# Two transformer layers on one core: order of the q/k remainders, score products and end-of-batch work in the first layer's attention

## The reference

```python
xn = layernorm(x)
# layer 0 attention: 16 heads of width 64
q, k, v = einsum('qdh,bcd->bhcq', Q, xn)*sq, einsum(..., K, xn)*sq, einsum(..., V, xn)*sv
p = softmax(causal(q @ k.T / 64))
z = einsum('dvh,bhcv->bcd', W, p @ v) * (sqrt(2) / 16)
# layer 0 ffn: a shared expert and 32 routed ones, the best 6 of a token weighted
f = sum_e comb[t, e] * (silu(xn @ gate_e.T) * (xn @ up_e.T)) @ down_e.T + shared(xn)
x = x + z + f
# layer 1: attention with 4 heads of width 32, and three 128-wide quantized
# linear blocks with layernorm and gelu
x = x + attn1(layernorm(x)) + ffn1(layernorm(x))
```

## Time and profile before

| what | value |
|---|---|
| median of 3 runs | 1194.93 us (1194.64 to 1196.25) |
| the profiled execution's own time | 1196.25 us |
| its span, first to last instruction | 1194.4 us |
| TensorE busy | 1173.1 us, 98% |
| VectorE busy | 981.5 us, 82% |
| ScalarE busy | 810.0 us, 68% |
| GpSimd busy | 405.4 us, 34% |
| mean granted TensorE clock | 0.997 of full speed |

### The profile page before, as it was taken

One profiled execution on the slowest core, in us unless ns is written; L12 is line 12 of the kernel. 1 busy time (PEld: TensorE's weight loads), 2 busy tenths in 40 slices (PEclk: granted clock), 3 DMA queues, 4 the chain that ended last, 5 costly groups with the idle time before them and its releaser, 6 DMA issues.

```text
span 1194.4 us, 23821 instructions
## 1 busy us (share of the span) xinstructions
PE 1173.1 (98%) x8908; PEld 898.2 (75%) x8908; DVE 981.5 (82%) x1918; ACT 810.0 (68%) x2182; POOL 405.4 (34%) x364
## 2 busy tenths in 40 slices
PE   8999999999999999999999999999999999999998
PEld 6777687767776777677767777777777777767866
DVE  5988588869886989698969886988797878988886
ACT  6885577557755775677567755775577668767775
POOL 1326420640064007300630064006400768526820
PEclk9999999999999999999999999999999999999999
DMA  7004200320031004100410041004100410000000
GB/s 261 2 30 144 90 1 30 125 62 2 30 125 63 1 30 128 60 1 30 131 56 2 30 134 54 2 30 134 53 2 30 144 43 2 10 10 19 1 11 28
DMA packets 44292, 63.93 MB, mean 54 GB/s; under 512 B 8144, under 2 KB 18384, under 8 KB 43920
## 3 DMA queue, kind: packets, MB, share of 16 engines
q1 hardware_dynamic: 44176, 62.39, 16.3%
HBM read 59.48 MB, written 2.88 MB: 52 GB/s over the span
## 4 chain that ended last, share of the span: by engine, by line
PE 81%; DVE 9%; ACT 4%; issue 2%; DMA 1%; POOL 1%; SPq 1%; DVEq 0%; POOLq 0%; ACTq 0%
PE psum L1507 14%; PE psum L1529 12%; PE psum L1454 12%; PE psum L65 10%; PE psum L67 9%; PE psum L66 9%; PE psum L1564 4%; DVE mneg L1146 3%; ACT probs L766 3%; PE psum L1464 2%; PE psum L1753 2%; PE psum L1533 1%; PE psum L1816 1%; DVE qk_lo L1126 1%; PE psum L1406 1%
## 5 line engine op out<-in xcount | busy, mean ns | idle before, releaser
L766 ACT ACTIVATE probs<-psum,mneg 128x256 f32<-128x256 f32 (+3 forms) x528 | 253.0, 495 | 166.3 <-DVE mneg L1146 165.4
L1146 DVE TENSOR_REDUCE mneg<-psum 128x2 f32<-128x1024 f32 (+2 forms) x320 | 245.2, 819 | 46.4 <-PE psum L1464 44.0
L1137 DVE COPY pt<-psum 128x512 f32<-128x512 f32 x320 | 204.8, 681 | 42.3 <-PE psum L1507 40.4
L1507 PE MATMUL psum<-ident,probs 128*128 128x128 f32 x1600 | 210.0, 277 | 3.9 <-DVE pt L1137 1.6
L1507 PEld LDWEIGHTS psum<-ident,probs 128*128 128x128 f32 x1600 | 177.1, 141 | 31.8 <-ACT probs L766 13.7
L573 POOL TENSOR_TENSOR qk_lo<-sg,qk_hi 128x512 fp32r<-128x512 f32 x64 | 91.8, 1441 | 163.0 <-ACT qk_hi L820 163.0
L1529 PE MATMUL psum<-pt,v_all 128*64 128x384 f32 (+5 forms) x1088 | 142.6, 412 | 0.0
L537 POOL TENSOR_TENSOR rstd<-var,mhalf 128x4 f32<-128x4 f32 x7 | 7.1, 1012 | 383.3 <-DVE var L1032 383.3
L1454 PE MATMUL psum<-qk_hi 64*128 64x512 f32 (+7 forms) x640 | 114.1, 352 | 5.4 <-DVE qk_lo L1131 3.6
L1529 PEld LDWEIGHTS psum<-pt,v_all 128*64 128x64 f32 (+1 forms) x1088 | 69.7, 135 | 63.0 <-issue 50.6
L65 PE MATMUL psum<-xt_hi,gu_hi 128*128 128x512 f32 x272 | 109.8, 404 | 1.3 <-DVE sg L1186 1.2
(11 more groups left out here) (276 smaller groups left out, 2503.2 us busy)
## 6 DMA issues: line engine op xcount, KB each, us to landing
crow<-weights SPq DMA_DIRECT2D x256, 128.0 KB, 2.9
rrow<-sums SPq DMA_DIRECT2D x128, 128.0 KB, 3.0
gu_raw<-in_gu SPq DMA_DIRECT2D x1, 2176.0 KB, 11.5
x_all<-in_x SPq DMA_DIRECT2D x8, 256.0 KB, 6.3
out_rows<-x_all SPq DMA_DIRECT2D x7, 256.0 KB, 2.3
down_raw<-in_down SPq DMA_DIRECT2D x1, 1088.0 KB, 13.6
wqkv_raw<-in_wqkv SPq DMA_DIRECT2D x1, 896.0 KB, 6.8
wqkv_raw<-in_wqkv SPq DMA_DIRECT2D x1, 512.0 KB, 5.0
```

The costliest lines, as they stand in the source:

```text
L766: last = act.activation(probs[:, h * HALF + PROB[t]:h * HALF + PROB[t] + w], bank[score_bank(rnd, c) + h][:, o:o + w], ACT.Exp, bias=mneg[ ...
L1137: dve.tensor_copy(turned_rows(rnd)[:, s % 2, :, 3 - s // 2, :], turn_bank(rnd, s).rearrange("p (j q) -> p j q", q=P)).then_inc(pt_ready, 1)
L1146: last = dve.tensor_reduce(mneg_h[:, :, t], psum[:, b:b + 2, o:o + P * (t + 1)], AX, ALU.max, negate=True)
L1507: last = nc.tensor.transpose(turn_bank(rnd, s)[:, i * P:(i + 1) * P], probs[:, v:v + P], ident[:, :])
```

## The change

- VectorE copies turned block 3 between the q and the k remainder, no longer behind both; it adds the rows of the batch before in pass 7, no longer in pass 6.
- TensorE makes chunk 2's products ahead of chunk 0's of the next pair. The wait for the copies of blocks 3 and 4 moves ahead with them, the wait for `qk_lo_ready` stays ahead of both.
- The accumulator of the batch before is turned in pass 7, behind blocks 0 to 2 and the wait for `copy_y`, into bank 6 (bank 7 for the last batch, whose rows are turned later).
- In pass 7 blocks 1 and 2 are turned within the slot; blocks 3 and 4 are turned between and behind the two half units of unit 0. The wait for the rows (`x1_ready`) goes from ahead of block 0 to ahead of the last value products.
- ScalarE's early load of the Silu table is taken out. The load itself is then placed where the first Silu stands.

```diff
         def rows_bank(b):
-            return bank[7]
+            return bank[6] if b < B - 1 else bank[7]
...
                     if p == PAIRS - 2:
                         copy_combt(b)
-                    if p == PAIRS - 1:
-                        load_table(ACT.Silu)
                     take_tile1(n)
...
                         rest_q(n + 2, SCALE0)
-                        rest_k(n + 2)
                     if p < PAIRS - 1:
                         take_turned(n, [3])
-                    if p == PAIRS - 2 and b:
+                    elif b:
                         add_rows(b - 1)
+                    if p < PAIRS - 2:
+                        rest_k(n + 2)
...
                 score_products(n, 1, n % 2, ROWS0, True).then_inc(scored, 1)
-                if p < PAIRS - 1:
-                    pe.wait_ge(qk_lo_ready, (n + 1) * 2 + 2)
-                    pe.wait_ge(exp_done, exp_count(n, 0))
-                    score_products(n + 1, 0, (n + 1) % 2, ROWS0)
                 if p:
                     pe.wait_ge(pt_ready, n * (TURNS - 1))
                     pe.wait_ge(pt4_ready, n)
+                if p < PAIRS - 1:
+                    pe.wait_ge(qk_lo_ready, (n + 1) * 2 + 2)
                 score_products(n, 2, n % 2, ROWS0)
+                if p < PAIRS - 1:
+                    pe.wait_ge(exp_done, exp_count(n, 0))
+                    score_products(n + 1, 0, (n + 1) % 2, ROWS0)
                 score_masks(n, 2).then_inc(scored, 1)
...
-                if p == PAIRS - 1:
-                    if b:
-                        pe.wait_ge(x1_ready, b)
-                    turn_step0(n, 0)
-                    return
                 for s in range(3):
                     turn_step0(n, s)
...
-                else:
+                elif p == PAIRS - 2:
                     pe.wait_ge(y_ready, n)
                     turn_weights(b)
-                    if b:
-                        pe.wait_ge(pt_ready, n * (TURNS - 1) + 1)
-                        turn_acc(b - 1)
-                turn_step0(n, 3)
-                turn_step0(n, 4)
+                elif b:
+                    pe.wait_ge(y_ready, n)
+                    turn_acc(b - 1)
+                if p < PAIRS - 1:
+                    turn_step0(n, 3)
+                    turn_step0(n, 4)
...
                 n = (b + 1) * PAIRS - 1
-                for s in range(1, TURNS):
-                    turn_step0(n, s)
-                project_unit(b, 0)
+                half_unit(b, 0, 0)
+                turn_step0(n, 3)
+                half_unit(b, 0, 1).then_inc(gu_done, 1)
+                turn_step0(n, 4)
                 pe.wait_ge(pt_ready, n * (TURNS - 1) + 3)
                 project_unit(b, 1)
+                if b:
+                    pe.wait_ge(x1_ready, b)
                 pe.wait_ge(y_ready, n)
                 weigh_pair(n)
```

## The result

The changed kernel takes 1216.24 us (median of 4 runs, 1215.68 to 1217.07) against 1195.12 us (median of 4, the three of the table and one more): 1.0176 times the time of before, 95% interval 1.0158 to 1.0194, or 21.1 us more. The forecast was 1213 with a range of 1199 to 1222, slower with a chance of 0.94. Its size was 18 us; the narrower span that it gave for its own mechanism, 1206 to 1215, was missed by 1.2 us.

A forecast was written before the change was run, and what follows sets the result against it. TensorE's instruction stream was taken to set the time. Terms of 13.0 and 5.0 us made 18.0, added to the profiled 1196.25 us for 1214.3, or 1213 on the median, range 1199 to 1222.

The forecast's parts named there:

- Part 1: Steady passes, VectorE order: k remainder 0.61 us later, TensorE waits for it in 48 passes; 13.0 us.
- The restart: TensorE after a stall in a steady pass: 0.06 us more between the first and second groups of products.
- Part 2: Steady passes, TensorE order: chunk 2's products ahead of the next pair's chunk 0 are worth nothing by themselves.
- Part 3: Turned accumulator moved from pass 6 to pass 7, batches 1 to 7: 0.98 less 0.26 us a batch, 5.0 us.
- Part 4: Other edits, including the rows' wait, half units in pass 7 and the late Silu table load: cost nothing.
- the cover of 0.4 us: Pass 7's end: unit 0's gate done at 332.8, TensorE needing it for unit 2 at 333.27; 0.4 us left.
- rival (b): Silu late after the table load: 0.9 us a batch falls on TensorE, 7 us more, 1220; chance 0.08.
- What would show it: Signs in the new profile: L1454's waits for L1131 grow from 8 to some 56, steady passes to about 8.6 us.
- (a): Steady passes: k remainder not late, as TensorE reaches the wait over 0.31 us later than modelled; 1200, chance 0.09.
- (d): Faster: pass 6 saves 0.26 us in 7 batches and neither new wait binds; 1193.1, chance 0.03.
- (e): Whole kernel: nothing changes because opposing terms cancel; 1195, chance 0.03.
- (c): Steady passes: no slack anywhere, each of 48 pays the full 0.61 us; 1229, chance 0.04.

The follow-up runs named there:

- The wait moved: Changed kernel with the k-remainder wait, in passes 1 to 6, ahead of chunk 0's products instead of chunk 2's: 1201.49 us, ratio 1.0062 to the kernel before.
- the VectorE order alone: Kernel before with one edit, VectorE copying turned block 3 between the q and k remainders: 1206.02 against 1195.89 us, ratio 1.0078.
- the score order alone: Kernel before with one edit, chunk 2's products and the waits for blocks 3 and 4 ahead of chunk 0's: 1208.68 against 1195.89 us, ratio 1.0106.
- the run that avoids it: Kernel before with the change's end of pass 7, but the accumulator turned behind the first half unit and block 3: 1196.67 against 1195.46 us, ratio 1.0010.

## Why the prediction was right, point by point

**What bounds the kernel** held: TensorE's stream, full in the steady passes, where any wait is paid at its full length.

**Part 1, 13.0 us.** The place, the mechanism and the number of passes held: remainder 0.6 us later, 6 passes in 8 batches, 8.62 us a pass against a forecast of 8.36 + 0.25. The wait moved takes 13.6 us away. That 0.25 met 0.26 is luck in part, for three small terms are off and cancel (medians of the steady passes). A pass swallows 0.17 us of lateness, not 0.12, since ScalarE's rounding of q also takes 0.60 us instead of 0.65. The restart is 0.04 us, not 0.06: with the VectorE order alone it is 1.38 us from the first product behind the wait to the value products, before 1.34. And TensorE starts 0.15 us behind the remainder's end, not 0.05, because this wait is written last. Where another wait is written behind it, as in the VectorE order alone, that last term is absent and a pass is 8.53 us; so that run cost 9 to 10 us, not 13.

**Part 2, nothing: wrong as a sentence by itself.** "So the swap itself is worth nothing" is refuted by the score order alone, 12.8 us. The 0.51 us that block 3's copy had to spare was spare time before 314.83, and the swap brings the need forward to 314.07 while the old VectorE order supplies it at 314.32. The text held only with the new VectorE order, for which its 313.72 was computed. What is true is that three things of VectorE (q remainder, k remainder, copy) must now all be done when TensorE comes to one place. Whichever is third is late, and putting VectorE's order back changes nothing (1216.21). In the changed kernel the third is the k remainder, so the sum did not suffer; for the score order alone the same text says nothing against 12.8 us measured.

**Part 3, 5.0 us.** Pass 6 went from 6.83 to 6.57 (forecast 0.26 less), pass 7 from 7.68 to 8.61 (0.93 more, forecast 0.98). The stall for y is 0.53 by the run that avoids it, forecast 0.54. By time the part costs 3.7 us (2.5 to 4.9), by the passes 7 x (0.93 - 0.26) = 4.7.

**Part 4, nothing: right in seven batches.** In batch 2 the Silu starts at 337.25 and the gate of unit 0 ends at 338.57. TensorE comes to unit 2 at 339.00, 2.36 us behind the start of the last value products as in the kernel before, so the cover of 0.4 us was there:

```profile
335.34 0.60 ACT L797 ACTIVATE pt<-psum 128x512 f32<-128x512 f32 x1 [3.02 <-PE psum L1506]
...
335.96 1.28 ACT L830 ACT_TABLE_LOAD   x1
...
337.25 1.08 ACT L830 ACTIVATE sg<-psum 128x512 f32<-128x512 f32 x2
...
339.00 0.48 PE L65 MATMUL psum<-xt_hi,gu_hi 128*128 128x512 f32 x1
```

In batch 0 it was not. There the gate ends 0.52 us later against the value products, as late as the rounding of the down weights put the load, and TensorE comes to unit 2 after 2.51 us. The forecast left out this ScalarE instruction, which only batch 0 has, and took the cost at nothing. It is 1.7 us in the trace and 3.5 by time, and the largest term that the forecast missed. By time the parts add up to 13.6 + 3.7 + 3.5 = 20.8 of 21.1 us, where the forecast had 13.0 + 5.0 + 0.

Behind a copy that is just over, the Silu starts 1.29 us after the table load's start. The Trainium skill, "ScalarE: Activation LUTs", section What ACT_TABLE_LOAD costs, gives a drain on top of that; this trace shows none here either, and rival (b), built on a slow load in every batch, fell.

**What would show it** named 56 waits of L1454 for L1131. The waits came, 48 of them, but under "issue".

**Rivals.** (a), (d) and (e) needed the remainder not to be late and fell with the 8.62 us passes; (c) fell as well, since the margins of 0.35 and 0.12 us counted.

## What to carry to other kernels

Where the bounding engine is full, ask of each wait not only whether it is met now but which operation of the supplier will be the last one needed at that place. An order on one engine and an order on the other have to be judged as a pair, and a wait belongs directly ahead of the instruction that reads the data: here the place of one wait is worth 13.6 of 21 us. And run a hidden cost through the one iteration that is unlike the others (here batch 0 with its weight rounding), as a cover of 0.4 us is gone with one extra instruction of 0.6.

## What the runs showed that was not expected

- Which of several waits is written last matters: a stall ended by the last one lets TensorE start 0.15 us behind the releasing operation's end, a stall ended by an earlier one 0.05 us, and a pass is 8.62 against 8.53 us. A wait that stands alone costs no more than the earlier one: the copy of y in pass 7 is followed after 0.05 to 0.06 us in all seven batches. The kernel before shows the slower start too, in its second layer: eight stalls ahead of transposes (L1507), where the wait for a copy is written behind that for the exponentials and ends last, have 0.14 to 0.15 us. Why this is so was not tried; in the steady passes the row of the slower one is put down to "issue".
- Four norm rows on VectorE take 1.10 us with GpSimd idle and 3.08 us while GpSimd subtracts two tiles (L573). The Trainium skill, "SBUF — State Buffer", section "SBUF: two separate sides", tells of a port that VectorE and GpSimd share; the trace agrees in that VectorE is held up, by 1.98 us here, while the first of the two subtractions takes 1.74 us and the second 1.29.
- The TensorE clock fell to half for 3.4 us at 115.9 us in the profiled execution of the kernel before; what TensorE did ahead of it was wait: 2.67 us busy of the 3.40 before. Such stretches are in some executions of a kernel and not in others, and are part of the scatter: on the four chips the executions of the kernel before with a mean granted clock of 0.997 took 1.1 to 2.6 us more on average than those with 1.000.
